# Four graph layers on one core: one DRAM table for states and sums, and an empty instruction ahead of every streamed indirect transfer

## The reference

```python
h = relu(layernorm(x)); x = x + gat2(h)    # two attention layers with self loops, 3 heads of 32, then 1 of 32, then @ Wf
h = relu(layernorm(x)); x = x + rgcn2(h)   # two relation layers, 8 relations: mean of x[src] per (dst, r) @ W[r] + x @ root
h = relu(layernorm(x))
f = 0.1 + h * (1 - h / 5) * (h - 1)        # "own" part of the third layer
x = x + f + segment_sum(weight * h[src] * h[dst] / (5 + 0.9 * h[src] + 0.1 * h[dst]), src)
h = relu(layernorm(x))
x = x + segment_sum(einsum(h[src], W_rel[type90]) * e, dst)   # e: a scalar from h[src], the attributes and h[dst]
```

## Time and profile before

| | us |
|---|---|
| median of 3 runs | 8152.44 (8133.22 to 8157.42) |
| the profiled execution | 8120.19 |
| its span | 8118.4 |
| VectorE busy / TensorE busy / POOL busy / ScalarE busy | 3659.3 / 3171.1 / 4266.3 / 1170.9 |
| mean granted clock of TensorE | 0.609 |

### The profile page before, as it was taken

How to read it: one execution, slowest core, us unless ns; L and a number is a source line. 1 busy time by engine, 2 the same in 40 slices (tenths; PEclk the granted TensorE clock), 3 DMA queues, 4 the chain that set the end, 5 groups by cost and what they waited for, 6 DMA issues and landing times. The chain is left out here.

```text
span 8118.4 us, 44641 instructions
## 1 busy us (share of the span) xinstructions
PE 3171.1 (39%) x13056; PEld 2436.8 (30%) x13056; DVE 3659.3 (45%) x8866; ACT 1170.9 (14%) x1912; POOL 4266.3 (53%) x3949
## 2 busy tenths in 40 slices
PE   5799999721245114510177213531111110111331
PEld 3587655420134113410166202431101110110221
DVE  8533699730266226740044204783424217312464
ACT  0344555410022013300011000100000000000000
POOL 5544455557500755057600574127888881677555
PEclk9765899855566555555566556665555555555666
DMA  1111222201000212110122101122222223210111
GB/s 35 32 46 46 62 67 67 69 8 9 9 14 28 51 25 59 60 20 14 21 89 97 43 17 40 58 72 34 47 26 49 23 15 127 75 19 18 34 44 52
DMA packets 283353, 350.10 MB, mean 43 GB/s; under 512 B 133518, under 2 KB 204432, under 8 KB 281970
## 3 DMA queue, kind: packets, MB, share of 16 engines
q1 hardware_dynamic: 112158, 295.24, 10.9%
q0 software_dynamic: 169376, 41.40, 6.3%
q10 hardware_dynamic: 1576, 10.60, 0.5%
HBM read 231.06 MB, written 122.29 MB: 44 GB/s over the span
## 5 line engine op out<-in xcount | busy, mean ns | idle before, releaser
L2092 POOL DMA_INDIRECT r_ring<-t_rel,idx x392 | 386.4, 986 | 728.9 <-POOLq L118 504.6
L1451 POOL DMA_INDIRECT g_ring<-t_gat,idx x392 | 400.1, 1021 | 648.5 <-POOLq L118 459.4
L2316 POOL DMA_INDIRECT acc<-l_rows,l_uniq x392 | 630.3, 1608 | 125.3 <-issue 114.4
L2302 POOL DMA_INDIRECT l_ring<-t_mix,idx x392 | 423.4, 1080 | 412.5 <-POOLq L118 293.4
L502 POOL DMA_INDIRECT pay<-in_x,gidx x392 | 440.5, 1124 | 375.4 <-DVE a_act_t L587 276.5
L1781 POOL DMA_INDIRECT r_ring<-t_rel,idx x392 | 398.9, 1018 | 403.2 <-POOLq L118 278.8
L2580 PE MATMUL ps_l<-w_rel,l_pick 128*128 128x256 f32 x784 | 260.3, 504 | 828.6 <-DVE l_pick L2609 765.5
L2539 POOL DMA_INDIRECT l_ring<-t_last,idx x392 | 397.8, 1015 | 330.0 <-ACTq L2534 207.0
L2357 PE MATMUL ps_l<-l_msg,l_alike 128*128 128x16 f32 x784 | 176.2, 375 | 988.3 <-DVE l_msg L2422 910.6
L774 POOL DMA_INDIRECT t_sort<-pay,c_pos x392 | 386.5, 986 | 312.8 <-DVE c_pos L840 211.6
L866 PE MATMUL ps_c<-plane,c_hit 128*128 128x400 f32 x1568 | 544.2, 500 | 2.3 <-ACT c_hit L792 2.3
(11 more groups left out here) (528 smaller groups left out, 8209.7 us busy)
## 6 DMA issues: line engine op xcount, KB each, us to landing
c_rows_d<-row_dst SPq DMA_DIRECT2D x98, 256.0 KB
l_keys<-row_at SPq DMA_DIRECT2D x49, 512.0 KB
l_typs<-row_typ SPq DMA_DIRECT2D x49, 512.0 KB
g_hs<-t_gat SPq DMA_DIRECT2D x30, 660.0 KB
acc<-r_zero SPq DMA_DIRECT2D x60, 320.0 KB
t_rel<-r_row SPq DMA_DIRECT2D x30, 640.0 KB
r_hs<-t_rel SPq DMA_DIRECT2D x30, 640.0 KB
d_gain<-acc SPq DMA_DIRECT2D x30, 640.0 KB
```

What stands on the lines that cost most here:

```text
L1451: pool.indirect_dma_start(ring[:, s % (NR * QN), :], None, t_gat2, bass.IndirectOffsetOnAxis(idx2[:, s:s + 1], 0)).then_inc(gat_in[s // BA ...
L2092: pool.indirect_dma_start(ring[:, s % (NR * QN), :], None, t_rel2, bass.IndirectOffsetOnAxis(idx2[:, s:s + 1], 0)).then_inc(gat_in[s // BA ...
L2302: pool.indirect_dma_start(ring[:, s, :], None, t_mix, bass.IndirectOffsetOnAxis(idx2[:, s:s + 1], 0)).then_inc(gat_in[s // BATCH], 16)
L2316: pool.indirect_dma_start(acc[r], bass.IndirectOffsetOnAxis(uniq[:, s:s + 1], 0), rows[:, (s // ES) % RR, s % ES, :], None, compute_op=ALU.add
```

## The change

1. `paced` ends with an empty instruction, so one stands ahead of each streamed transfer: 56 + 336 + 392 + 392 + 392 + 16 + 392 + 393 = 2369 of them on POOL.
2. A single table `acc` takes the place of the two `acc`, of `t_last` and of `fin`. Every table now has its slot part ahead of its dense part; the index constants follow, two operations on VectorE changing their kind.
3. Relation pass 1 zeroes only the 128 spare rows, and VectorE waits for gathers per 8 columns, not per 40.
4. Relation pass 2 does `own` after each block's finish, from the row in SBUF, and SP stores the state with f added into `acc`, 30 stores of 320 KB. TensorE waits for gathers per 16 columns.
5. In the third layer the loads and `own` are gone, AHEAD is 16, and each scatter-add waits for the landing of the one right before it.
6. The stage of 15 windows is gone.
7. The last layer loads the 400 slot columns of `acc` in 5 windows and takes their normalisation for the scalars of `h[dst]`; it gathers raw states and normalises them per 40 columns. The scatters wait for all gathers and all five loads, and go into `acc` itself, whose dense part is then the output's source.

```diff
...
+DENSE = P * SLOTS
...
         engine.wait_ge(landing[n], 16 * BATCH)
+    engine.nop(nofuse=True)
...
-    t_last = scratch("t_last", (P * ROWS, FEAT))
-    acc = [scratch(f"acc_{r}", (P * ROWS + P, FEAT)) for r in range(2)]
-    fin = scratch("fin", (NP + P * (T + 1), FEAT))
+    acc = scratch("acc", (P * ROWS + P, FEAT))
...
-        return table[0:P * ROWS].rearrange("(p r) f -> p r f", r=ROWS)[:, lo:lo + n, :]
+
+        if lo < SLOTS:
+            return table[0:DENSE].rearrange("(p r) f -> p r f", r=SLOTS)[:, lo:lo + n, :]
+        return table[DENSE:P * ROWS].rearrange("(p c) f -> p c f", c=C)[:, lo - SLOTS:lo - SLOTS + n, :]
...
-                    nc.gpsimd.iota(home[:], pattern=[[1, C]], base=SLOTS, channel_multiplier=ROWS,
+                    nc.gpsimd.iota(home[:], pattern=[[1, C]], base=DENSE, channel_multiplier=C,
...
+                            sp.dma_start(acc[P * ROWS:P * ROWS + P], zero[:]).then_inc(zeroed, 16)
...
-                            if setup:
-                                for a in acc:
-                                    sp.dma_start(columns_of(a, QN * n, QN), zero[:].rearrange("p (q f) -> p q f", f=FEAT)
-                                                 ).then_inc(zeroed, 16)
...
-                                all_landed(dve, gat_in, QN * i, QN * i + w)
+                            all_landed(dve, gat_in, c0, c0 + ES)
...
+                        hold(sp, own_ok, n + 1)
+                        sp.dma_start(columns_of(acc, columns(n), QN), state(n)).then_inc(own_out, 16)
...
-                        if s == 0:
-                            all_landed(pe, gat_in, QN * i, QN * i + widths[i])
+                        if s % 2 == 0:
+                            all_landed(pe, gat_in, QN * i + ES * s, QN * i + ES * (s + 2))
...
+                        h, xc = row[:, n % 2], state(n)
+                        ln_back(step, h, t).then_inc(row_ok, 1)
                         dve.wait_ge(row_ok, n + 1)
+                        step.link(v.tensor_scalar(grow[:], h, -1.0 / 5.0, 1.0, ALU.mult, ALU.add))
+                        step.link(v.tensor_tensor(grow[:], grow[:], h, ALU.mult))
+                        step.link(v.scalar_tensor_tensor(grow[:], h, -1.0, grow[:], ALU.add, ALU.mult))
+                        v.scalar_tensor_tensor(xc, grow[:], 0.1, xc, ALU.add, ALU.add).then_inc(own_ok, 1)
+                        dve.wait_ge(own_ok, n + 1)
...
-            AHEAD = 2 * QN
+            AHEAD = 2 * ES
...
-                        if s >= 2:
-                            pool.wait_ge(scat[r], 16 * (s // 2))
-                        pool.indirect_dma_start(acc[r], bass.IndirectOffsetOnAxis(uniq[:, s:s + 1], 0),
+                        if s:
+                            pool.wait_ge(scat, 16 * s)
+                        pool.indirect_dma_start(acc, bass.IndirectOffsetOnAxis(uniq[:, s:s + 1], 0),
                                                 rows[:, (s // ES) % RR, s % ES, :], None, compute_op=ALU.add
-                                                ).then_inc(scat[r], 16)
+                                                ).then_inc(scat, 16)
...
-                        for n in own_at.get(e, []):
-                            if n + 2 < NCH:
-                                own(n + 2)
...
-                            for r in range(2):
-                                act.wait_ge(scat[r], 16 * (ES // 2) * (e - RR + 1))
+                            act.wait_ge(scat, 16 * ES * (e - RR + 1))
...
-                        if e % (QN // ES) == 0:
-                            i = e // (QN // ES)
-                            all_landed(dve, gat_in, QN * i, QN * i + widths[i])
+                        all_landed(dve, gat_in, ES * e, ES * (e + 1))
...
-                            sp.dma_start(gain[:, k % 2, r], columns_of(acc[r], WQ * k, WQ)).then_inc(in_s[k % 2], 16)
...
-                        sp.dma_start(columns_of(t_last, WQ * k, WQ), row[:, k % 2]).then_inc(out_s[k % 2], 16)
...
-                        step.link(v.tensor_tensor(xc, xc, gain[:, b, 0], ALU.add))
-                        step.link(v.tensor_tensor(xc, xc, gain[:, b, 1], ALU.add))
...
-                        ln_front(step, xc, t[b]).then_inc(var_ok, 1)
...
-                        pool.indirect_dma_start(ring[:, s, :], None, t_last,
+                        pool.indirect_dma_start(ring[:, s, :], None, acc,
...
-                    pool.wait_ge(dense_out, 16)
+                    all_landed(pool, gat_in, 0, T)
+                    for k in range(NW):
+                        pool.wait_ge(x_in[k], 16)
...
-                        pool.indirect_dma_start(fin, bass.IndirectOffsetOnAxis(home_i[:, s:s + 1], 0),
+                        pool.indirect_dma_start(acc, bass.IndirectOffsetOnAxis(home_i[:, s:s + 1], 0),
...
-                    all_landed(pool, gat_in, 0, T)
 
                 @block.sync
                 def _(sp):
-                    sp.dma_start(fin[0:NP].rearrange("(p c) f -> p c f", c=C), XD[:]).then_inc(dense_out, 16)
+                    for k in range(NW):
+                        sp.dma_start(X[:, WQ * k:WQ * (k + 1)], columns_of(acc, WQ * k, WQ)).then_inc(x_in[k], 16)
...
-                                 fin[0:N].rearrange("(p c) f -> p (c f)", c=C)).then_inc(copied, 16)
+                                 acc[DENSE:DENSE + N].rearrange("(p c) f -> p (c f)", c=C)).then_inc(copied, 16)
...
+                    def front(k):
+                        hold(dve, x_in[k], 16)
+                        ln_front(step, X[:, WQ * k:WQ * (k + 1)], t[k % 2]).then_inc(var_ok, 1)
+
+                    front(0)
+                    for k in range(NW):
+                        if k + 1 < NW:
+                            front(k + 1)
+                        part = t[k % 2]
+                        step.link(v.scalar_tensor_tensor(dot[:], part["cent"], 0.0, bcast(c_row[:, 2:3, :], [P, WQ, FEAT]),
+                                                         ALU.max, ALU.mult))
+                        to = v_dst[:, WQ * k:WQ * (k + 1)]
+                        step.link(v.tensor_reduce(to, dot[:], AX_X, ALU.add))
+                        hold(dve, root_ok, k + 1)
+                        step.link(v.reciprocal(part["root"], part["root"]))
+                        step.link(v.tensor_tensor(to, to, part["root"], ALU.mult))
+                    dve.sem_inc(vdst_ok, 1)
...
+                    def edge_front(i):
+                        w = widths[i]
+                        all_landed(dve, gat_in, QN * i, QN * i + w)
+                        part = {"sum": te["sum"][:, 0:w], "var": te["var"][:, 0:w], "cent": te["cent"][:, 0:w],
+                                "sq": te["sq"][:, 0:w]}
+                        ln_front(step, ring[:, QN * i:QN * i + w], part).then_inc(var_ok, 1)
...
+                        edge_back(i)
...
+                        if i + 1 < NE:
+                            edge_front(i + 1)
...
```

136 lines of the change are left out of this document (38 added, 98 removed).

## The result

The changed kernel took 8203.13 us in the median of 6 runs (8162.23 to 8225.51), the kernel before 8141.13 (6 runs, 8119.06 to 8157.42): ratio 1.0089, 95% interval 1.0065 to 1.0113. It is slower by about 0.9%, where 6620 had been forecast.

The account below looks back on a forecast made before the run. It took TensorE completions arriving late while POOL streams waiting indirect transfers as the bound. Terms -35 -330 -240 -420 -300 +40 +70 -203 -115 = -1533 gave 6587, or 6620 for the median; range 6480 to 8120, this case's own 6470 to 6900.

Parts of the forecast that it names:

- the first of the change's parts: Early gathers and four stages: empty instructions take the transfers' waits and relieve late completions; -35, -330, -240, -420, -300 us.
- the copy at 5563.35: Third layer: a ScalarE copy still waited 44.5 us, 17 us after scatters and gathers began to alternate; noted as slightly against.
- the first-16-gathers contrast: Early gathers: ScalarE's step takes 6.42 us beside 16 gathers without waits; the next two steps take 46.0 us beside waiting gathers.
- The stages without the delay: Both attention layers and relation passes 1 and 2, relieved: 578 for 907, 628 for 868, -420, and 600 for 904 us.
- The last layer: Last layer: gathers cover VectorE's added 110 us, and the 122.0 us of scatters waiting on VectorE go; -115 us.
- Empty instructions: 2369 empty instructions on POOL, 0 to 0.09 us each, free where another engine sets the stage; +40 us.
- The windows: The stage of 15 windows goes whole; -203 us.
- Third layer: Third layer: +25 waiting for the first copy, +25 waiting between scatter-adds, +20 in the tail; +70 us, bounds +40 and +160.
- My argument against: Against the slower scatter chain: scatter-adds wait for a landing nowhere near the end now, since two are in flight.
- the 3.6 that I had worked out and set aside: Scatter-add landing: about 2.0 us fixed cost put behind an issue of 1.6; counted from the issue's start it would be hidden.
- Own part in relation pass 2: Relation pass 2: four added VectorE operations, 3.1 us a block, 93 in all, counted within its -300; stores cost nothing.
- the third, the scatter chain without relief: Third layer: no relief, landing later than a POOL pair, 376 pairs x 0.3 = 113 us; 8230 (8165 to 8400), chance 0.10.

Follow-up runs that it names:

- e14: Changed kernel with gathers paced differently by stage and in four ways in the last layer, half its products dropped from sub-block 30 on: 7970.53 us beside 8126.85.
- e2: Kernel before with only an empty instruction added ahead of each streamed transfer: 6591.06 us beside 6603.66, ratio 0.9997.
- e13: The change unaltered against the kernel before, on a chip without the delay: 6553.93 us beside 6590.69, ratio 0.995.
- e5: The change unaltered, timed again against the kernel before on a chip with the delay: 8186.68 us beside 8114.69, ratio 1.0076.
- e7: The change with third-layer scatter-adds going to two tables in turn, half of the sums not reaching the state: 8033.3 us, ratio 0.9914 to the kernel before.
- e8: The change without the four own operations per block in relation pass 2, stores kept: 8127.72 us, ratio 1.0018 to the kernel before.
- e6: Kernel before with 16 gathers ahead of the third layer's scatter-adds instead of 80, and gather waits per 8 columns: 8140.98 us, ratio 1.0016.

## Why the prediction was wrong

**The step that failed** is the first of the change's parts, with its reading of the profile: "what hurts is ... a long row of indirect transfers that each carry a wait. An empty instruction ahead of each takes the wait". The changed kernel's stages and its products at 44.8 show that nothing was relieved; e14's relation pass 1, with a wait on one gather in eight, took 1029 for 1028. The waits were innocent. The forecast had put -1325 on this part, and the five stretches together gave +71. The observation behind it was sound, that a delay sits in the stages from 1722 on and isn't work: e2's stages, the same kernel without it, are 1470 us shorter in sum. But I took it for a property of the program alone, and it appears on some chips and not on others. The rows that I had from one profile don't tell these apart; what could have held me back was the copy at 5563.35, which I had noted as speaking against the wait, and the first-16-gathers contrast, which an allowance that runs down would explain as well. I gave 0.62 to a mechanism that rested on two contrasts.

**The stages without the delay** were sized well, though nothing in the change brings them about: forecast 578, 628, about 608 and 600; e13 has 589, 631, 597 and 588. The last layer: forecast 1069, e13 1043. That is no merit of the forecast's mechanism: it had the size of the delay, not what removes it.

**Empty instructions**, +40: nothing that can be told on chips without the delay, 0.995 with and 0.994 without them, and 0.9997 in the kernel before. With the delay they were not measured by themselves.

**The windows**, -203: right, on both kinds of chip.

**Third layer**, +70, bounds +40 to +160: measured +142 in the first pair, 1445 - 1302 = +143 in e5, 1446 - 1296 = +150 without the delay. The term was mis-sized in its wait per pair, 0 to 0.3 us and 25 in the sum: it is 0.34 (3.53 for 3.19) and 128. With the tail the chain costs 151 by e7, for which I had 45. My argument against, that scatter-adds wait for a landing nowhere near the end, looked at the landing of the one two before and says nothing of the one before; the DMA slice after the last scatter-add bounded the last packet, not the signal. The Trainium skill, page "DMA: Bandwidth & Descriptors", section "Anatomy of one DMA — SWDGE (gpsimd) path", says that most of the fixed 2 us is the receipt of the write, which comes after the packets; by that, the trace's packets end too early to price a wait. The measured 3.37 us from one scatter-add to the next in the tail, 1.54 of it issue, lies near the 3.6 that I had worked out and set aside.

**Own part in relation pass 2** cost 48 in the first pair, 59 to 70 by e8, and 7 without the delay. **The last layer** cost +33 in the first pair, +23 on e5's chip (1211 for e6's 1188), and +16 without the delay, instead of -115. The 122 us that the scatters waited for VectorE were to go with the stall; in the changed kernel on the first chip they are 137.4, and in e2 and e13 none. The added work of VectorE is hidden where it keeps pace with POOL and comes on the path where it lags.

**The rivals.** What came to pass on the first chip is the third, the scatter chain without relief, which I gave 0.10 at 8230 (8165 to 8400): 8203. The chain's place and sign were right. Its price with the tail, 151, was larger than the 113 + 20 named. No rival had that the delay might be absent from the kernel before. The rule that I had quoted from the Trainium skill, page "SBUF — State Buffer", section "Who interferes with whom", that TensorE and ScalarE wait on no one, forecast no relief and was right in that. It is about access to SBUF, and it neither forecasts nor explains the delay, which stands in rows 3 and 4 and is gone from e2.

Why the sign turns: without the delay -203 stands against +150 for the chain, +7 and +16: -30, and e13 has -37. With it the own part takes 48 to 70 and the last layer 23 to 33, so that the parts come to +10 to +43 while the medians differ by +62 and +72. The rest isn't explained: stages that the change hardly touches vary between traces of the same code by as much (the counting sort's first scatter comes between 910.7 and 980.2 us, the second attention layer takes 862 to 892), and what the empty instructions cost there is not known.

**What stays open**: what makes a chip delay events while POOL streams, whether it is the chip or something else that lasted as long as a group; whether in relation pass 2 the rests or the slower stream kept it away, and why they didn't end it in the last layer; what the empty instructions cost with it; and whether the change with rests would beat both kernels there. Of the kernels here none beat the kernel before on both kinds of chip: the change alone wins 0.5% on one and loses 0.8% on the other; e7's two tables took 0.9914 of it on the chip with the delay, but without half of the sums.

## What to carry to other kernels

Before a stall is put down to the program, time the unchanged program on another chip: here the kernel before took 6604 us on one and 8141 on another, which no view of one profile shows. A chain of read-modify-write transfers to one table costs the time to the landing signal, 3.1 to 3.4 us after the start here, not the time to the last packet; a second table hides it, and is worth the pass that adds both up only if that pass costs less than the chain (here the pass cost 203 us and the chain 150). Work moved to an engine that seems hidden is priced by whether that engine keeps pace in that stage: the same 93 us cost 7 on a chip without the delay and 48 to 70 with it.

## What the runs showed of the hardware that had not been expected

- Of the chips met, some ran the kernel before in medians of 6582 to 6604 us and some in 8115 to 8141. The difference lies in stages in which POOL streams indirect gathers or scatters at one per 1.25 us beside other engines' work (585 for 907, 629 for 868, 605 for 1028, 581 for 904, 1027 for 1184). The third layer, where scatter-adds and gathers alternate and one comes per 1.65 us, is the same (1296 for 1302), and so is the counting sort (685 for 685), where 392 scatters take 655 us. A gather's median on POOL is 0.944 us on both.
- On a chip with the delay, waited-for events can pass as slowly as one per 1.4 us while POOL issues a transfer each 1.25 us: 44.8 us for a sub-block of 32 TensorE instructions, and in one stretch 1.40 us between VectorE's own linked operations, though 0.32 in others. With a rest after each eight gathers from the stage's start it didn't appear (634 us for 952), and with one transfer in flight, one per 2.6 us, it ended within 26 us.
- A scatter-add's landing is signalled 3.1 to 3.4 us after its start, while the DMA engines' last packets were seen 2.4 us or a little more after it.
- The granted clock in the first stage varied from run to run (0.70 and 0.73 over it in the two first profiles, 0.77 in e2), and with it the stage's length: 949, 915 and 893 us.
